# Taking out the four waits that hold routing scatters behind the shared expert

## Time and profile before

| | us |
|---|---|
| median of 3 runs | 1290.65 |
| lowest and highest of the 3 | 1285.19, 1294.76 |
| the profiled execution, whole | 1291.12 |
| its span | 1289.3 |
| PE busy | 1183.4 |
| DVE busy | 904.1 |
| ACT busy | 866.1 |
| POOL busy | 667.3 |

### The profile page before, as it was taken

How to read it: one execution, slowest core, us unless ns; L and a number is a source line. 1 busy time by engine, 2 the same in 40 slices (tenths; PEclk the granted TensorE clock), 3 DMA queues, 4 the chain that set the end, 5 groups by cost and what they waited for, 6 DMA issues and landing times.

```text
span 1289.3 us, 25190 instructions
## 1 busy us (share of the span) xinstructions
PE 1183.4 (92%) x7600; PEld 834.3 (65%) x7600; DVE 904.1 (70%) x2657; ACT 866.1 (67%) x2320; POOL 667.3 (52%) x746
## 2 busy tenths in 40 slices
PE   4899999999999999999999999999767898989985
PEld 1565776766766666666676766676533586778963
DVE  3787788789789879979988987887754332222336
ACT  3998789878878877887887887788452332323413
POOL 4564333345645565555655556565546233444557
PEclk9999999999999999999999999999978999999998
DMA  7686677877876555564465465356345488898676
GB/s 267 164 212 135 127 132 141 169 159 165 198 159 147 120 110 110 104 120 97 92 124 105 78 122 113 76 95 117 61 125 152 126 230 220 219 240 215 143 197 208
DMA packets 394759, 190.01 MB, mean 147 GB/s; under 512 B 317521, under 2 KB 373303, under 8 KB 394625
## 3 DMA queue, kind: packets, MB, share of 16 engines
q1 hardware_dynamic: 375040, 173.53, 58.7%
q0 software_dynamic: 16416, 11.70, 5.0%
q10 hardware_dynamic: 3168, 3.15, 0.7%
HBM read 75.32 MB, written 64.69 MB: 109 GB/s over the span
## 4 chain that ended last, share of the span: by engine, by line
PE 62%; issue 9%; DMA 9%; POOL 7%; DVE 5%; ACT 5%; another core or an unknown queue 2%; SPq 1%; POOLq 0%; ACTq 0%; DVEq 0%
PE bank L1079 14%; PE bank L1108 13%; PE bank L1123 10%; DMA Y<-W,wix 8%; PE bank L1094 7%; PE bank L1140 7%; PE bank L1172 4%; POOL BUF L757 3%; PE bank L1248 2%; PE bank L1261 2%; POOL P L1009 1%; PE bank L1207 1%; POOL PH L1014 1%; DMA X<-in_x 1%
## 5 line engine op out<-in xcount | busy, mean ns | idle before, releaser
L1350 ACT ACTIVATE P<-bank,nm 128x256 f32<-128x256 f32 x512 | 237.8, 471 | 95.7 <-DVE nm L1519 93.3
L1079 PE MATMUL bank<-RB,W 128*128 128x512 f16 x1076 | 275.4, 381 | 1.4 <-DVE RB L471 1.4
L1108 PE MATMUL bank<-RB 128*128 128x256 f32 x1024 | 243.9, 381 | 12.0 <-issue 7.2
L757 POOL DMA_INDIRECT BUF<-RT,ix x192 | 197.3, 1028 | 79.3 <-issue 44.4
L1009 POOL TENSOR_SCALAR P<-P,rr 128x256 f32<-128x256 f32 x256 | 124.4, 497 | 208.5 <-DVE rr L1501 204.5
L1108 PEld LDWEIGHTS bank<-RB 128*128 128x128 f32 x1024 | 184.5, 190 | 39.0 <-issue 9.1
L1079 PEld LDWEIGHTS bank<-RB,W 128*128 128x128 f16 x1076 | 105.7, 98 | 118.3 <-issue 2.5
L1519 DVE TENSOR_REDUCE nm<-bank 128x2 f32<-128x512 f32 x256 | 173.8, 680 | 5.6 <-PE bank L1108 5.3
L1014 POOL TENSOR_TENSOR PH<-P,PH 128x512 f16<-128x512 f32 x86 | 104.3, 1212 | 111.4 <-ACT PH L1366 111.1
L1140 PE MATMUL bank<-W,O 128*128 128x256 f16 x1060 | 157.8, 273 | 1.6 <-DVE O L1525 1.6
L1030 POOL DMA_INDIRECT Y<-W,wix x64 | 90.9, 1420 | 121.6 <-ACT W L1430 78.9
(11 more groups left out here) (223 smaller groups left out, 1989.4 us busy)
## 6 DMA issues: line engine op xcount, KB each, us to landing
RB<-in_ewT SPq DMA_DIRECT2D x24, 352.0 KB
BUF<-zrow SPq DMA_DIRECT2D x24, 321.0 KB, 3.5
W<-BUF SPq DMA_DIRECT2D x64, 120.4 KB
HT<-in_ewT SPq DMA_DIRECT2D x18, 352.0 KB
HT<-in_wc SPq DMA_DIRECT2D x24, 256.0 KB, 4.6
HT<-in_ws SPq DMA_DIRECT2D x24, 256.0 KB, 5.1
Y<-zrow SPq DMA_DIRECT2D x20, 256.0 KB
RB<-in_ewd SPq DMA_DIRECT2D x24, 176.0 KB
```

The lines of the kernel that those rows point to most:

```text
L757: eng.indirect_dma_start(BUF, bass.IndirectOffsetOnAxis(ap=ix[:, rt, t, k:k + 1], axis=0), RT[:, rt, t, :], None, bounds_check=CAP * E - 1 ...
L1079: r = eng.matmul(bk_[:, :], W[:, m, a, c * 2048 + h * 128:c * 2048 + (h + 1) * 128], XT[:, bp % 2, b, c, :], start=(k == 0), stop=(k == n ...
L1108: r = eng.matmul(bS[u % 2][:, t * 256:(t + 1) * 256], QK[:, i % 2, 0, q * 256 + t * 128:q * 256 + (t + 1) * 128], QK[:, i % 2, 1, q * 256: ...
L1350: r = eng.activation(P[:, u % 2, t * 256:(t + 1) * 256], bS[u % 2][:, t * 256:(t + 1) * 256], ACT.Exp, bias=nm0[:, u % 4, t:t + 1], accum_ ...
```

## The change

The table of waits is emptied. The four scatters no longer wait for `saf`; their waits on `po` and `bi`, the order of POOL's queue and all else stay.

```
-REST = {(6, 11): 2, (6, 18): 5, (7, 8): 9, (7, 16): 12}
+REST = {}
```

## The result

| | before | after |
|---|---|---|
| median, us | 1292.70 (4 runs, 1285.19 to 1299.44) | 1310.49 (4 runs, 1306.42 to 1311.48) |
| the profiled execution, us | 1291.12 | 1310.04 |
| first expert's work on PE, us | 1033.5 | 1054.3 |

The change makes the kernel slower: ratio 1.0159, 95% interval 1.0115 to 1.0202, that is +17.8 us in the medians and +18.9 in the profiled executions. The forecast was +8.3, with the right sign and within its range, but less than half of what came.

A forecast was written before the change was run, and what follows sets the result against it. It took PE to bound the kernel (92% busy, 62% of the chain), with scatters costing by what they delay. Direct effect 0, second batch pair +4.7, first +3.6 gave +8.3 us, so 1299 us; range 1280 to 1312.

The forecast's parts named there:

- The direct effect of 0: Tail: scatters ending earlier gain 0 us, since nothing late waits for them.
- the fourth wait does nothing: Wait number 8 of batch pair 7 on `saf` holds nothing in the profiled execution, so its burst is already 16 long.
- The mechanism: Tail: a long burst of scatters beside working PE makes PE's completions late, 0.46 to 1.04 us per us of burst.
- nothing changes: Rival: the stall is not the scatters' doing or comes once whatever the burst's length; 1290.6 us, chance 0.28.
- Faster: the stall goes away: Rival: the second burst starts on empty queues and its stall vanishes; -11.0 us, 1279.6, chance 0.15.
- The second batch pair: Burst from 979.25 us: 8 more scatters, 10.2 us, join the burst that already stalls; +4.7 us, bounds 0 and +10.6.
- at 0.46: Lower rate, from the burst of 16: 9.3 us of PE idle for 20.2 us of burst; the forecast used it.
- upper rate of 1.04: Rate from the burst of 16: the chain's 21.0 us put to no engine, per us of burst.
- The first batch pair: Burst from 930.12 us now runs 16.0 us beside working PE; half of +7.3 us taken, +3.6, bounds 0 and +16.6.
- the full price or near it: Rival: each us of burst beside working PE holds the chain 1.04 us; +27.2 us, 1317.9; over +12.9 had chance 0.17.
- PE falls behind 2 to 3 us past the end of the burst: Second burst: ACT's waits for PE last until 2 to 3 us after its end, near 1012 plus earlier losses.
- The rule weighed against it: Skill page: only DVE and GpSimd contend for a port, PE never waits there, so scatters cannot hold PE; 1290.6 us.

The follow-up runs named there:

- e1: Kernel before with only the waits of batch pair 6 taken out, those of batch pair 7 kept: 1300.76 us, ratio 1.0078.
- e4: One scatter left for each of the last two batch pairs, 46 of the last 48 left out: 1274.69 us, ratio 0.9867 against the kernel before.
- e8: 46 of the last 48 scatters replaced by a POOL subtraction each, 0.69 us long: 1277.43 us, ratio 0.9914 against the kernel before.
- e9: Changed kernel with one memset of 304 elements on POOL behind each of the last 48 scatters: 1281.69 us, ratio 0.9904 against the kernel before.
- e10: Changed kernel with one memset of 16 elements on POOL behind each of the last 48 scatters: 1311.89 us, ratio 1.0139 against the kernel before.
- e2: Kernel before with only the waits of batch pair 7 taken out, those of batch pair 6 kept: 1298.85 us, ratio 1.0070.
- e15: Changed kernel with SP's loads of experts 7 to 16 held until the shared expert's product 17: 1332.57 us, ratio 1.0337 against the kernel before.
- e7: Changed kernel with every index of the last 48 scatters out of bounds, so no row is moved: 1314.77 us, ratio 1.0203 against the kernel before.
- e6: Changed kernel with all rows of the last 48 scatters written to a spare array: 1311.67 us, ratio 1.0187 against the kernel before.

## Why the prediction was right in sign and wrong in size

**The direct effect of 0** held: nobody waited for the scatters. The gather even came 20.8 us later than before (1043.81), for the index it needs was late. **The bursts** of 24 at 1.28 us came as said. That **the fourth wait does nothing** was not tried alone; e1's profile shows only that such a wait can be met before POOL comes to it.

**The mechanism** held against its strongest counter, that the one stall was a coincidence (*nothing changes*): e4 and e8 take the scatters away and the stall goes, e9 spaces them and it goes, e10 does not and it stays. *Faster: the stall goes away* fell too: the burst started 30 us after the one before and stalled for 20.0 us of PE rather than 9.3.

**The second batch pair**, a term of +4.7, measured +7.9 by e2 and +10.7 by the stretches of the changed kernel. The step was "at 0.46". The rate isn't constant: over a burst of 20.2 us it was 0.46, over one of 30.9 it was 0.65. The 8 scatters that joined cost (20.0 - 9.3) / 10.2 = 1.05 us each us, which is the upper rate of 1.04 that I had set aside (by e2's 7.9 us it is 0.77). The rows fit this reading: once signals are late, PE uses up its work in store, and each further us is lost in full. My reason for the lower rate, that PE has work in store, then holds for the burst's first part only.

**The first batch pair**, a term of +3.6, measured +9.8 (e1) to 11.5. The step that failed is "I take half": the burst of 7 at the same place, which showed 0, was too short to say anything of one that runs on for 16.0 us behind PE's start. Beside that, the place was wrong. I looked for ACT waiting for PE; it was DVE waiting for its own signals. A chain of ten dependent steps of 0.16 us pays the lateness at eight of its nine distances: 9.2 us until `RT`, and PE behind it idle for 8.90. And the sum had no term for the clock: at 0.52 behind that idle time PE lost another 3.0 us, so that this pair's part is 12.0 us by the rows. This is the larger part of the missing 9.5 us, and even the lower rate in full, 7.3, would have been short.

**The sum**: +12.0 in full at the lower rate was too little, +27.2 too much; 17.8 measured. That lies in the rival of the full price or near it (over +12.9), which I gave 0.17, and not in the forecast's part. **"PE falls behind 2 to 3 us past the end of the burst"** held: the last late signal reached ACT at 1024.52, 2.5 us after the last scatter's end at 1022.02.

**The rule weighed against it**: PE had no gap for 24.00 us beside a POOL that reads and writes SBUF, and stood 20.0 us beside POOL's indirect DMAs. The Trainium skill, page SBUF — State Buffer, section SBUF: two separate sides, says that PE waits for nobody at SBUF's ports. As to ports e8 agrees. What the changed kernel shows does not look like a port: ACT began the SiLU of part 12 at 1024.52, though the matmuls before it are modelled to end at 1006.79, and PE had gone on with the next ones meanwhile. Of late signals that rule says nothing; taken as "POOL can't delay PE" it would have given 1290.6 where 1310.5 was measured.

**Open**: which path the signals share with the scatters' descriptors. That the scatters' messages together with those of the other engines exceed a fixed rate, so that a backlog grows and drains, would fit: a sharp edge between 1.28 and 1.51 us, fours as good as single pauses, late steps that go on while PE stands, late starts on PE itself. It is argued, not shown. Nor is it shown what sets the start: the first late step came 18.3 us into the first burst, but the second burst of e15 meets one within 5.8 us. Plain DMAs issued by POOL at this pace were not tried, so it is open whether the DMA being indirect matters. Whether the effect would be as large without the profile's recording was not tried.

## What to carry to other kernels

A run of indirect DMAs from POOL is not free because POOL is: look at the chain for pieces put to no engine beside it, and at small dependent steps that stand further apart than their length. Brake it by pace (here 1.51 us rather than 1.28, one memset each, 1281.7 us against 1291.1 before), not by waits on the progress of what it disturbs, and look at what stands behind it in POOL's queue. When a rate is taken from one short stretch, ask what its first part had in store; the rest may cost in full.

## What the runs showed of the hardware

- Indirect DMAs of 128 rows issued every 1.28 us beside working PE made signals late, with the DMA engines at a share of 0.04 (first burst) or 0.35 (second). ACT's longest waits that ended with such a signal lasted 14.3 us (changed kernel) to 17.1 (e10). At 1.51 us nothing was late, at 1.39 only PE's signals.
- In the first burst nothing was late for 14.5 us with PE nearly idle; the first late step came 3.9 us after PE's restart (944.81 to 948.7). The steps stayed late for 5.4 us after PE had stopped (953.14 to 958.52). With PE at work, the chain's first piece put to no engine begins 4.4 us after the burst's start in the second burst (991.27 to 995.65), and in e15 0.5 us after it (996.59 to 997.07). That the work of PE is what was missing before 944.81 fits this, and no run tests it alone.
- Starts of matmuls that waited for nothing named in the profile were late too: up to 2.1 us apart in e2.
- After 8.90 us of doing nothing PE ran 5 us at a granted clock of 0.52, and its 12 matmuls took 5.20 us rather than 2.75.
- It needs neither rows that land (e7), nor rows left out (e6), nor other loads beside the burst (e15), and POOL's own work does not bring it about (e8).
- A POOL operation of 0.12 us fits between two scatters and leaves their pace at 1.28 us; one of 0.36 us makes it 1.51, one of 0.25 us 1.39.
